# Writing out one engine's loop over pairs of groups: TensorE's passes one behind the other

## Chip, core and metric

The kernel runs on one core of a Trainium2 chip. The metric is the device time of the whole program in microseconds (us): median 2250.71 us of three runs, 2248.42 to 2252.54.

The engines of a core are TensorE (PE; its weight loads are shown apart as PEld), VectorE (DVE), ScalarE (ACT), GpSimd (POOL) and SyncE (SP, which here only issues transfers). Each has an instruction stream of its own; they meet in semaphores.

## What is computed

Four graph layers on 128 boards of 64 tokens with 256 features, everything in float32. Before each layer: layer norm, then ReLU; after each: a residual.

```
h = relu(layernorm(x));  x = x + attention8(h, adj)     # 8 heads, six with static masks, two with adj|eye
h = relu(layernorm(x));  x = x + attention4(h, adj)     # 4 heads, all masked by adj
h = relu(layernorm(x));  x = x + gated(h, adj)          # 4 heads: tanh(where(adj, e @ Wh.T, 0)) @ Wh, relu, gate
h = relu(layernorm(x));  x = x + attention4(h, adj)

attention(h):  softmax(where(mask, q @ k.T * scale, -big)) @ v @ Wo + bo
gated(h):      ha = relu(A @ Wh) @ A_w.T;  hf = h @ fc_w.T
               c = sigmoid(hf @ g1_w.T + ha @ g2_w.T + gbias);  hf * c + ha * (1 - c)
```

## The kernel before

Four boards (256 tokens) are a group, so there are 32 groups. Two groups are in work at once, in two slots: slot 0 takes the even groups, slot 1 the odd ones. A pair of groups is one turn, and there are ITERS = 16 turns. The big matrix products are made of three products of rounded halves (w_hi, w_lo and the same split of the activations), which is why TensorE has so many matmuls; all of them come from one helper line, 437, the transposes from 505, 581 and 714.

What one group goes through is a list of 109 steps (STEPS): for each of the four layers bn, stats, norm, turn (transposes), q, k, v, scores, softmax, and so on; the gated layer (number L2) has r, e, h, s2, a, ah, hp, ha, hf, hat, g, sum. Every engine walks through this list in a function of its own, `step(slot, what, counts)`, and does its share of the step. The two slots are out of phase: slot 1 lags by some 50 steps. How many steps of slot 1 follow each step of slot 0 on an engine is a table written by hand (ORDER).

`passes` runs this on an engine. Its inner `turn` does one pass over the 109 steps of slot 0 and, mixed in, the last `lag` steps of slot 1's group before and the first ones of its group now. The first turn is written out. The other 15 are a hardware loop, `eng.Fori`, in which the semaphore values to wait for depend on the turn and sit in registers (`Counts` with `eng.snap`; register arithmetic, recorded under many lines, works them out). After the loop the rest of slot 1's last group is written out. The five engines each have such a loop, and the code of a turn on TensorE is by far the longest.

The place at which a turn of TensorE ends and the next one begins matters here: the last thing in a turn is step r of the gated layer in slot 1 (six matmuls ps<-hT,u_vec), the first in the next are steps e (matmuls ps<-hT,w_hi and ps<-hT,w_lo), of slot 1 too. At that time slot 0 ends its group: VectorE writes the finished rows (line 1028, into xn), SyncE then issues the transfer of x for the slot's next group (line 350) and the store of the finished one (line 380), and VectorE's bn (line 931) reads the new x. From bn the chain goes over stats (lines 938, 941), the power on GpSimd (line 410) and norm (line 949) to TensorE's transposes (line 505).

The names: hT is the activation after norm and ReLU, transposed; wide holds e; rs and row_terms are small terms of the gated layer; probs the attention's probabilities; xn the normed rows or, at the end of a group, the result; ps is PSUM.

Of the kernel before, what the change touches and what calls it, by code (L numbers as in the profile page):

```python
# [62 lines left out]
def constants():  # L63
# [22 lines left out]
    for part in (0, LO):  # L86
# [13 lines left out]
ORDER = {  # L100
# [5 lines left out]
    "act": (57, (  # L106
# [33 lines left out]
def build(nc, x_in, adjq_in, adjt_in, mats_in, cols_in, rows_in, cst_in, out):  # L140
    GROUPS = x_in.shape[0] // TOK
    ITERS = GROUPS // SLOTS
# [6 lines left out]
    with ctx:  # L149
# [153 lines left out]
                       ("g", L2, 0), ("g", L2, 1), ("sum", L2, 0)])  # L303
        STEPS = att_steps(0) + att_steps(1) + L2_STEPS + att_steps(2)

        def passes(eng, step, order):

            n = len(STEPS)  # L310
            lag, merge = order
            assert len(merge) == n and sum(merge) == n

            def turn(first, now, before):
                done = 0
                for k in range(n):
                    step(0, STEPS[k], now)
                    for done in range(done + 1, done + merge[k] + 1):
                        if done > lag:
                            step(1, STEPS[done - lag - 1], now)  # L320
                        elif not first:
                            step(1, STEPS[n - lag + done - 1], before)

            turn(True, Counts(0), None)
            if ITERS > 1:
                with eng.Fori(0, ITERS - 1) as i:
                    turn(False, Counts(i + 1, eng.snap), Counts(i, eng.snap))
            last = Counts(ITERS - 1)
            for k in range(n - lag, n):
                step(1, STEPS[k], last)  # L330
# [63 lines left out]
        def _(pool):  # L394
# [33 lines left out]
            for s in range(SLOTS):  # L428
                last = nc.gpsimd.memset(RS[s][:, 0:TOK].bitcast(F32), 0.0)
            last.then_inc(setup["terms_zero"], 1)  # L430
            passes(pool, step, ORDER["pool"])


        @block.tensor
        def _(pe):
# [285 lines left out]
            def step(s, what, v):  # L721
# [3 lines left out]
                else:  # L725
                    att(s, k, a, i, v)

            passes(pe, step, ORDER["pe"])


        @block.scalar
        def _(act):
# [32 lines left out]
            def att(s, k, a, i, v):  # L765
# [12 lines left out]
                elif k == "v":  # L778
                    act.wait_ge(sm["v_ps"], n)
                    fn(V[s][:, :, :], bank(s, 3), ACT.Copy).then_inc(sm["v_sb"], 1)  # L780
                elif k == "max":

                    u, m, j, cj = i
                    act.wait_ge(sm["rowmax"], v.eight[u])
                    for b in range(NB):
                        at, row = (cj * NB + b) * SQ, m * NB + b
                        p = PR[s][:, j, at:at + SQ]
                        last = fn(p, p, ACT.Exp, bias=ROWMAX[s][:, row:row + 1], accum_out=ROWSUM[s][:, row:row + 1])  # L788
                    last.then_inc(sm["exp"], 1)
                elif k == "pt":  # L790
                    act.wait_ge(sm["pt_ps"], v.six[2 * a + i])
                    us = turned(a)[i]
                    _, _, j, cj = us[0]
                    at = slice(cj * TOK, (cj + len(us)) * TOK)
                    fn(PTS[s][:, j, at], bank(s, 1 - i)[:, at], ACT.Copy).then_inc(sm["pt_sb"], 1)
                elif k == "pv":
                    act.wait_ge(sm["o_ps"], v.six[2 * a + i])
                    fn(OT[s][:, 0, i, :].rearrange("p (t e q) -> p t e q", t=TT, e=2), o_view(s, i), ACT.Copy
                       ).then_inc(sm["oT_hi"], 1)
# [55 lines left out]
            def step(s, what, v):  # L855
# [3 lines left out]
                else:  # L859
                    att(s, k, a, i, v)  # L860

            passes(act, step, ORDER["act"])


# [275 lines left out]
```

## Time and profile before

| | before |
|---|---|
| median of three runs | 2250.71 us (2248.42 to 2252.54) |
| the profiled execution | 2248.06 us, its span 2245.9 us |
| TensorE busy (matmuls) | 2011.9 us, 21228 matmuls |
| VectorE, ScalarE busy | 1445.6 us, 1151.8 us |
| mean granted TensorE clock | 0.967 |
| instruction fetch (queue q8) | 190 packets, 3.11 MB |
| loop turns (15) | 169.3 to 2179.7 us |

A span goes from the first to the last instruction. In lists of groups the words behind the bar are busy time and mean duration, then the idle time before such instructions and what ended it; "issue" is put where the profile sees nothing that was waited for. The granted clock is 1.00 at 2.4 GHz and 0.50 at 1.2 GHz; between these it is the mean of a stretch that has both. A branch at the end of a loop is recorded with its own duration on the sequencer of each engine ("PEldq" is TensorE's).

### The profile page before, as it was taken

To read this page: it belongs to the slowest core of one execution; us is meant where nothing else is said; L and a number is where in the kernel's file an instruction comes from. 1 tells how busy PE (TensorE), PEld (TensorE's weight loads), DVE (VectorE), ACT (ScalarE), POOL (GpSimd) and SP (SyncE) were. 2 spreads that over 40 slices of the span, in tenths; PEclk is the share of its full clock that TensorE was granted. 3 is DMA by queue.
4 is the path that set the end of the run, shared out by engine and by line. 5 is a ranking of instruction groups with operands and counts; after the bars stand their busy time and mean duration, and the time that the engine had idled before them with its cause. 6 is when DMAs were issued, how large, how long until landed. Compare 5 with 4: busy or idle time off the path is not lost.

```text
span 2245.9 us, 53566 instructions
## 1 busy us (share of the span) xinstructions
PE 2011.9 (90%) x21228; PEld 1818.6 (81%) x21228; DVE 1445.6 (64%) x3769; ACT 1151.8 (51%) x3862; POOL 192.2 (9%) x203
## 2 busy tenths in 40 slices
PE   6699989899898989989899998989989899998997
PEld 5588878788887888878788887888888788887885
DVE  4466667667666667667666666666757666666663
ACT  3355555455455555555455454545455455455552
POOL 0000101100001100100110000100101100000100
PEclk8799999999999999999999999999999999999998
DMA  5000000000000000000000000000000000000000
GB/s 174 1 3 12 12 12 12 11 5 9 12 12 12 11 11 2 11 12 11 12 11 2 12 11 12 11 11 2 11 12 11 11 12 2 12 11 12 11 6 5
DMA packets 40630, 30.66 MB, mean 14 GB/s; under 512 B 15664, under 2 KB 40240, under 8 KB 40432
## 3 DMA queue, kind: packets, MB, share of 16 engines
q1 hardware_dynamic: 40432, 27.48, 4.1%
q8 instruction: 190, 3.11, 0.6%
q14 instruction: 8, 0.07, 0.0%
HBM read 19.08 MB, written 8.39 MB: 12 GB/s over the span
## 4 chain that ended last, share of the span: by engine, by line
PE 62%; issue 18%; DVE 12%; ACT 4%; POOL 4%; DMA 1%; DVEq 0%; SPq 0%; POOLq 0%; ACTq 0%
PE ps L437 57%; PE ps L505 4%; POOL small L410 3%; DVE small L931 2%; DVE xn L949 2%; PE ps L581 2%; ACT probs L788 1%; DVE x L1028 1%; DVE wide L1053 1%; DVE f L1062 1%; POOL x L423 1%; DVE aT L870 1%; ACT f L824 1%; ACT wide L816 1%; DVE small L938 1%
## 5 line engine op out<-in xcount | busy, mean ns | idle before, releaser
L437 PE MATMUL ps<-hT,w_hi 128*128 128x256 f32 x2560 | 511.2, 291 | 55.8 <-issue 47.7
L437 PEld LDWEIGHTS ps<-hT,w_hi 128*128 128x128 f32 x2560 | 420.5, 194 | 73.1 <-issue 50.8
L788 ACT ACTIVATE probs<-probs,small 128x64 f32<-128x64 f32 x1024 | 342.1, 339 | 33.2 <-DVE small L1009 31.4
L437 PE MATMUL ps<-hT,w_lo 128*128 128x256 f32 x1280 | 343.1, 288 | 0.0
L437 PEld LDWEIGHTS ps<-hT,w_lo 128*128 128x128 f32 x1280 | 249.2, 195 | 2.7
L437 PE MATMUL ps<-w_hi,hT 128*128 128x256 f32 (+1 forms) x1024 | 249.1, 312 | 0.0
L410 POOL TENSOR_TENSOR small<-small,consts 128x2 f32<-128x2 f32 x128 | 88.8, 694 | 1776.2 <-DVE small L941 1776.2
L437 PE MATMUL ps<-w_hi,oT 128*128 128x256 f32 x768 | 189.2, 311 | 27.4 <-DVE oT L870 27.4
L437 PE MATMUL ps<-wide,w_hi 128*128 128x256 f32 x1024 | 213.1, 285 | 0.2
L788 ACT ACTIVATION_READ_ACCUMULATOR probs<-probs,small 128x1 f32 x1024 | 196.2, 192 | 0.0
L816 ACT ACTIVATE wide<-ps,c_vec 128x256 fp32r<-128x256 f32 x256 | 107.6, 472 | 148.3 <-PE ps L437 148.3
L437 PEld LDWEIGHTS ps<-w_hi,hT 128*128 128x128 f32 x1024 | 175.4, 188 | 8.4
L1053 DVE SCALAR_TENSOR_TENSOR wide<-ps,c_vec,wide 128x256 fp32r<-128x256 f32 x256 | 109.5, 479 | 103.6 <-ACT wide L816 103.5
L437 PEld LDWEIGHTS ps<-w_hi,oT 128*128 128x128 f32 x768 | 147.5, 211 | 32.5 <-DVE oT L870 32.3
L437 PEld LDWEIGHTS ps<-wide,w_hi 128*128 128x128 f32 x1024 | 163.4, 188 | 3.1 <-DVE wide L870 0.7
L949 DVE TENSOR_SCALAR xn<-x,small 128x256 f32<-128x256 f32 x256 | 123.3, 523 | 62.0 <-POOL small L410 59.7
L437 PE MATMUL ps<-w_hi,cT 128*128 128x256 f32 x768 | 159.3, 290 | 0.3 <-ACT cT L848 0.3
L505 PE MATMUL ps<-consts,xn 128*128 128x128 f32 x512 | 116.3, 324 | 46.1 <-DVE xn L949 42.9
L437 PE MATMUL ps<-w_lo,hT 128*128 128x256 f32 (+1 forms) x512 | 149.9, 310 | 0.0
L763 ACT ACTIVATE hT<-ps 128x256 fp32r<-128x256 f32 x256 | 88.4, 383 | 98.5 <-PE ps L505 97.6
L505 PEld LDWEIGHTS ps<-consts,xn 128*128 128x128 f32 x512 | 62.5, 151 | 86.9 <-DVE xn L949 74.2
L437 PE MATMUL ps<-wide,w_lo 128*128 128x256 f32 x512 | 131.8, 280 | 0.0
(123 smaller groups left out, 4342.5 us busy)
## 6 DMA issues: line engine op xcount, KB each, us to landing
raw_mats<-mats SPq DMA_DIRECT2D x8, 1024.0 KB, 11.9
x<-x SPq DMA_DIRECT2D x32, 256.0 KB, 3.0
out<-xn SPq DMA_DIRECT2D x32, 256.0 KB, 3.0
adj<-adjq SPq DMA_DIRECT2D x64, 16.0 KB, 2.0
adjT<-adjt SPq DMA_DIRECT2D x64, 8.0 KB, 2.1
raw_consts<-board_consts SPq DMA_DIRECT2D x1, 451.5 KB, 3.1
raw_rows<-rows SPq DMA_DIRECT2D x1, 256.0 KB, 4.5
bias_cols<-cols SPq DMA_DIRECT2D x1, 6.0 KB, 3.6
```

The lines of the kernel that those rows point to most:

```text
L410: nc.gpsimd.tensor_tensor(RSTD[s], VE[s], HALF.broadcast_to([P, TT]), ALU.pow).then_inc(sm["rstd"], 1)
L423: nc.gpsimd.tensor_tensor(X[s][:, :], X[s][:, :], F[s][:, 0:512], ALU.add).then_inc(sm["x_ha"], 1)
L437: return nc.tensor.matmul(o, lhsT, rhs, start=start, stop=stop, skip_group_check=True)
L505: last = nc.tensor.transpose(bank(s, H_BANKS[c])[:, t * P:t * P + P], XN[s][:, t * D + c * P:t * D + c * P + P], IDENT)
L581: last = nc.tensor.transpose(bank(s, 1 - i)[:, at:at + P], PR[s][:, j, at:at + P], IDENT)
L763: fn(HT[s][:, 0, c, :], bank(s, H_BANKS[c])[:, 0:TOK], ACT.Relu).then_inc(S[s]["hT_hi"], 1)
L788: last = fn(p, p, ACT.Exp, bias=ROWMAX[s][:, row:row + 1], accum_out=ROWSUM[s][:, row:row + 1])
L816: last = fn(e_view(s, 0, oc, i), e_bank(s, E_BANKS[i], oc), ACT.Identity, bias=CVEC[:, oc, i:i + 1])
L824: fn(tanh_buf(s, i), bank(s, 2 + i), ACT.Tanh).then_inc(sm["tanh"], 1)
L931: nc.vector.bn_stats(STATS[s][:, t, :], X[s][:, t * D:t * D + D]).then_inc(S[s]["bn"], 1)
L949: ts(XN[s][:, t * D:t * D + D], X[s][:, t * D:t * D + D], MV[s][:, t, 0:1], RSTD[s][:, t:t + 1], ALU.subtract, ALU.mult).then_inc(S[s]["xn ...
L1053: stt(e_view(s, 1, oc, i), e_bank(s, E_BANKS[i], oc), CVEC[:, oc, i:i + 1], e_view(s, 0, oc, i).bitcast(F32), ALU.add, ALU.subtract).then_ ...
```

## The change

`passes` gets an argument. For TensorE the 15 turns behind the first are written out one behind the other by a loop in Python; the semaphore values of each turn are then constants. The other four engines keep their hardware loops.

```diff
-        def passes(eng, step, order):
+        def passes(eng, step, order, unrolled=False):
...
             turn(True, Counts(0), None)
-            if ITERS > 1:
+            if unrolled:
+                for i in range(1, ITERS):
+                    turn(False, Counts(i), Counts(i - 1))
+            elif ITERS > 1:
                 with eng.Fori(0, ITERS - 1) as i:
                     turn(False, Counts(i + 1, eng.snap), Counts(i, eng.snap))
             last = Counts(ITERS - 1)
...
-            passes(pe, step, ORDER["pe"])
+            passes(pe, step, ORDER["pe"], unrolled=True)
```

TensorE's program goes from 1367 rows of the listing to 10256, and its lines move by 3 (437 is 440 now). On the other four engines no row differs but for the line numbers.

TensorE at the end of a turn of the loop, before; what stands behind the branch is the code after the loop, and the branch goes back to the same steps of the next turn:

```order
L437 MATMUL ps<-bias_rows,sel_rows 128x256
L437 MATMUL ps<-hT,u_vec 36x256 [waits hT_hi_1]
L437 MATMUL ps<-hT,u_vec 36x256
L437 MATMUL ps<-hT,u_vec 36x256 [waits hT_hi_1]
L437 MATMUL ps<-hT,u_vec 36x256
L437 MATMUL ps<-hT,u_vec 36x256 [waits hT_lo_1] x2
L326 REGISTER_ALU
L326 COMPARE_AND_BRANCH
L437 MATMUL ps<-hT,w_hi 128x256
L437 MATMUL ps<-hT,w_lo 128x256
```

The same place now, where the second turn ends and the third begins:

```order
L440 MATMUL ps<-bias_rows,sel_rows 128x256
L440 MATMUL ps<-hT,u_vec 36x256 [waits hT_hi_1]
L440 MATMUL ps<-hT,u_vec 36x256
L440 MATMUL ps<-hT,u_vec 36x256 [waits hT_hi_1]
L440 MATMUL ps<-hT,u_vec 36x256
L440 MATMUL ps<-hT,u_vec 36x256 [waits hT_lo_1] x2
L440 MATMUL ps<-hT,w_hi 128x256
L440 MATMUL ps<-hT,w_lo 128x256
L440 MATMUL ps<-hT,w_hi 128x256
```

The register addition and the branch between the turns are no longer there; the matmuls and their waits stand as they did.

Inside a turn, on TensorE before step scores (q times k) of slot 0, before the change:

```order
L437 MATMUL ps<-w_lo,hT 128x256
L437 MATMUL ps<-w_hi,hT 128x256 x2
L560 REGISTER_ALU
L437 MATMUL ps<-kT,qT 64x64 [waits q_sb_0,k_sb_0]
L437 MATMUL ps<-kT,qT 64x64 x15
```

Such register rows, which work out the value of a wait, are gone in the same way at all places of the turn.

## Rows read from the trace of the kernel before

**Rows 1.** The page, busy time and share of the span by engine.

```profile
PE 2011.9 (90%) x21228; PEld 1818.6 (81%) x21228; DVE 1445.6 (64%) x3769; ACT 1151.8 (51%) x3862; POOL 192.2 (9%) x203
```

**Rows 2.** What TensorE waited for: total us, times, longest; then the group.

```profile
PE ps L437 <- issue: 50.0, 18, 3.8
...
L437 PE MATMUL ps<-hT,w_hi 128*128 128x256 f32 x2560 | 511.2, 291 | 55.8 <-issue 47.7
```

**Rows 3.** Line 326 (the loop): count, ns min/median/max, first and last start.

```profile
L326 PEldq COMPARE_BRANCH  x15: 83/3434/3934, 299.0 to 2179.7; - x15
...
L326 ACTq COMPARE_BRANCH  x15: 40/45/45, 295.2 to 2176.0; - x15
...
L326 DVEq COMPARE_BRANCH  x15: 50/56/67, 305.3 to 2182.5; - x15
```

**Rows 4.** DMA queues, 573 to 701.6 us: packets, MB, share of 16 engines.

```profile
q8 instruction: 10, 0.16, 0.5%
```

**Rows 5.** Five turns of the loop: stretch, length, busy by engine (instructions), clock, DMA.

```profile
169.30:299.00 129.70, 121.67 (x1319) 110.22 (x1317) 89.06 (x235) 70.68 (x240) 11.86 (x12) 0.99 0.03 10
299.00:435.20 136.20, 124.07 (x1317) 112.83 (x1316) 88.97 (x235) 70.79 (x240) 11.85 (x12) 0.96 0.03 10
435.20:568.50 133.30, 121.74 (x1319) 110.08 (x1317) 88.97 (x235) 70.67 (x240) 11.85 (x12) 0.99 0.04 10
...
967.90:1100.40 132.50, 120.52 (x1319) 108.81 (x1317) 88.96 (x235) 70.50 (x240) 11.86 (x12) 1.00 0.04 10
1100.40:1237.50 137.10, 125.17 (x1319) 113.89 (x1317) 89.13 (x235) 70.81 (x240) 11.85 (x12) 0.95 0.03 10
```

**Rows 6.** Timeline around the end of turn 3: start, us, engine, line, idle before.

```profile
567.90 0.87 PE L437 MATMUL ps<-hT,u_vec 128*36 128x256 f32 x6
...
568.81 0.47 ACT L811 ACTIVATE rs<-ps,s 36x256 fp32r<-36x256 f32 x1 [2.60 <-PE ps L437]
568.94 0.38 SPq L350 DMA_DIRECT2D x<-x  x1
...
572.08 0.36 PE L437 MATMUL ps<-hT,w_hi 128*128 128x256 f32 x1 [3.31 <-issue]
...
573.79 0.84 ACT L816 ACTIVATE wide<-ps,c_vec 128x256 fp32r<-128x256 f32 x2 [4.51 <-PE ps L437]
...
574.66 0.88 DVE L1053 SCALAR_TENSOR_TENSOR wide<-ps,c_vec,wide 128x256 fp32r<-128x256 f32 x2 [4.88 <-ACT wide L816]
...
575.45 0.74 DVE L931 BATCH_NORM_STATS2 small<-x 128x6 f32<-128x256 f32 x2
...
578.15 0.87 PE L505 MATMUL ps<-consts,xn 128*128 128x128 f32 x4
```

**Rows 7.** Timeline around the entry of the loop, in the same form.

```profile
168.79 0.86 PE L437 MATMUL ps<-hT,u_vec 128*36 128x256 f32 x6
169.49 0.36 PE L437 MATMUL ps<-hT,w_hi 128*128 128x256 f32 x1
...
169.83 0.40 SPq L350 DMA_DIRECT2D x<-x  x1
...
172.86 0.74 DVE L931 BATCH_NORM_STATS2 small<-x 128x6 f32<-128x256 f32 x2
...
175.56 0.87 PE L505 MATMUL ps<-consts,xn 128*128 128x128 f32 x4
```

**Rows 8.** Tile x on SyncE, 560 to 2200 us: from issue to landing.

```profile
DMA to landing us min/median/max: 2.8/3.0/3.7
```

**Rows 9.** Stretches around the ends of turns 3 and 8, in the form of rows 5.

```profile
563.00:568.50 5.50, 4.92 (x56) 4.57 (x56) 2.89 (x11) 1.80 (x5) 0.69 (x1) 0.69 0.00 0
572.00:578.00 6.00, 5.92 (x48) 5.76 (x48) 3.08 (x10) 2.52 (x6) 0.69 (x1) 1.00 0.05 17
...
1241.30:1247.00 5.70, 5.59 (x34) 5.62 (x35) 2.35 (x8) 1.68 (x4) 0.69 (x1) 0.70 0.01 4
1300.00:1309.00 9.00, 6.87 (x69) 5.99 (x68) 5.73 (x19) 3.29 (x15) 0.69 (x1) 0.81 0.00 0
```

## The prediction, made before the changed kernel ran

> **What bounds the kernel now.** I read the page first. TensorE is busy for 90% of the span, VectorE for 64%, ScalarE for 51%, so the time is TensorE's work plus the moments in which it has none [rows 1]. Then I read what TensorE waited for. The largest item is no other engine: 50.0 us are put down to issue, in 18 waits, and 47.7 us of it stand before one group of matmuls, the hT,w_hi ones [rows 2]. The reader is to see that "issue" here names no semaphore: nothing that the profile follows was late.
>
> The third view says where they sit. The branch that ends a turn of the loop (line 326) is recorded on each engine, 15 times. On ScalarE and VectorE it takes 40 to 67 ns each time. On TensorE it takes 83 ns once, the median is 3434 ns and the longest is 3934 ns [rows 3]. The loop has 15 turns, so 14 branches are taken and the last falls through; the one cheap record is the one not taken. The window of a turn that starts 4.5 us after its branch still has 10 instruction packets (0.16 MB) [rows 4]: some engine streams its code all the time, in a body that it runs again and again. By its length that is TensorE, with 1319 matmuls and 1317 weight loads in a turn beside 240 instructions on ScalarE and 235 on VectorE [rows 5]. So I read the stall as the wait for the block of code to which the branch goes back.
>
> **The change part by part.** Removed: 14 taken branches of TensorE, its register arithmetic, and the counter of its loop. Added: no matmul, no wait; the number of matmuls is the same. The other four engines keep program and order. So I need the price of a boundary with a branch, and of one without.
>
> Both are in the trace. At 567.90 TensorE starts its six u_vec matmuls, the last work of a turn, and the first matmul of the next turn, hT,w_hi, starts at 572.08: 4.18 us [rows 6]. At the entry of the loop the same two groups meet without a taken branch, since the code runs straight into the body: 168.79 and 169.49, 0.70 us [rows 7]. The difference is 3.48 us; times 14 that is **48.7 us**, and it agrees with the 47.7 us of issue and with the branch records.
>
> Is that time on the path? Behind the gap the next turn starts with the e matmuls of slot 1, which wait for nobody in the gap; ScalarE had done its last work (rs, 568.81 + 0.47) and sat idle for 4.51 us until TensorE gave it e, VectorE for 4.88 us [rows 6]. Nobody uses the gap. What is next in line is the transfer of x: issued at 568.94, read by VectorE's bn (L931) at 575.45, 6.51 us later; without the gap that is 3.03 us. Such a transfer lands 2.8 to 3.7 us after its issue, 3.0 in the median [rows 8]. So the cover of x is gone, and it is late by 0 to 0.67 us. At the loop's entry, where this distance is 3.03 us too (169.83 to 172.86), bn ran 3.37 us after hT,w_hi and the transposes (L505) 6.07 us after it, and at 572 also 3.37 and 6.07 [rows 6, 7]: there x was in time. I take 0.1 us on average, near the median, so **-1.5 us** in 14 turns; the ends are 0 and -9.4 us. The store of the finished group, which has to land before norm overwrites XN, moves with it in the same way and cost nothing at the entry, where norm and the transposes weren't late; I put it at 0.
>
> Register arithmetic: whatever it costs TensorE must be in the issue time that isn't before hT,w_hi, 50.0 - 47.7 = 2.3 us [rows 2]. Ends 0 and 2.3 us; I take 0, since these instructions run ahead of a queue of matmuls.
>
> The turns themselves give the other term. Turn 1, which no taken branch opens, takes 129.7 us. Nine turns with a stall take 132.5 to 133.3 us, which is 129.7 + 3.4. Five take 136.2 to 137.1 us, at a granted clock of 0.95 or 0.96 in place of 0.99 [rows 5]. All 14 turns from 299.0 to 2179.7 are 1880.7 us [rows 3]. The extra time of the five is clock. A short turn drops to 1.2 GHz once, in the stretch of single waits before its end (563.0 to 568.5, clock 0.69), and is at 1.00 behind the stall. A long one does the first too, but shows 0.70 right behind the stall (1241.3 to 1247.0) and 0.81 once more in the middle (1300 to 1309) [rows 9]. The lost part is 5.7 x 0.30 = 1.7 us and 9.0 x 0.19 = 1.7 us: 3.4 us per long turn. In front of the first stands the idle of the stall; TensorE busy across the boundary has no reason for it. The second comes in a quiet place of the softmax and appears only in turns that have the first. If all of it goes, 14 turns cost 14 x 129.7 = 1815.8 us, 64.9 us less than now; so the clock's part is 64.9 - 48.7 = **16.2 us** of gain. Its lower end is 0. It can't be excluded that a turn meets two half-speed stretches for other reasons, since the quiet places remain; I keep 3 us of it for two such turns: 13.2 us.
>
> Sum: 48.7 + 13.2 - 1.5 = 60.4 us. The profiled execution took 2248.06 us (span 2245.9 and 2.2 around it), 2.6 below the median of 2250.71. 2248.06 - 60.4 = 2187.7, and on the scale of the median 2190 us.
>
> One rule is against this. The trace has 83 ns for a branch not taken and 3434 ns for the median of TensorE's [rows 3]. The Trainium skill, Advanced Engine Details and Errata, section Control Flow Timing, puts a compare-and-branch at about 108 ns; by that the edit is worth 14 x 0.108 = 1.5 us in place of 48.7. The three other engines agree with the page's order of size; TensorE doesn't.
>
> **The rivals.** *The long turns stay.* The gap goes, but the half-speed stretches arise as often as now, from the quiet places alone: gain 48.7, less 1.5 for x: 2250.7 - 47.2 = 2203.5. For it: the middle stretch isn't at the boundary. Against: turns of both kinds have the same work, and what precedes the extra stretch is the stall. Chance 0.22.
>
> *The other side of the clock, and x.* The new turn of 129.7 us meets a second half-speed stretch each time (14 x 1.7 = 24 us), or x is late by its maximum (9.4): 2250.7 - 64.9 + 23.8 = 2210, with both 2219. Against it: turn 1 has the new form and shows neither. Chance 0.10.
>
> *The stall isn't the branch's.* TensorE would have to wait at this place for its code in any case, and the gap returns as a fetch in straight code: time as before, 2245 to 2251. For it: a price of a tenth of a microsecond for branches elsewhere [rows 3]; the page named above gives that result. Against: the entry at 169.3, where the same body is reached without a branch and without a gap [rows 7]. Chance 0.03.
>
> *Slower.* Straight code is never used twice, so every block of it must come from memory in time: 10 in most of a turn [rows 4], 140 in 14 turns. If each exposed a wait, the gain of 60.4 us is eaten from 60.4 / 140 = 0.43 us per block on; at 1 us per block the kernel takes 2250.7 - 60.4 + 140 = 2330. Against: such blocks are fetched now as well, in the same order, and all that is put down to issue outside the group behind the branch is 2.3 us in the whole span [rows 2]. The Trainium skill, Runtime: NRT & Kernel Launch, section Instruction fetch mechanics, calls the crossing of a block "mostly hidden"; the trace agrees, with those 2.3 us. Chance 0.02.
>
> **How the numbers follow.** My case has 0.60: 2190 us, its own range 2180 to 2199 from the bounds of x (-8), the register work (+2) and the clock (3 back, or a turn with no half-speed stretch, like the one of 132.5 us at clock 1.00, some more). 0.03 are left for below. The range for 8 in 10 takes in the first rival: 2178 to 2208. Something within 0.2% (4.5 us) of 2250.7, about what a measurement of this kernel can tell from no change, has 0.03; slower by more 0.02; faster 0.95.
>
> **What would show it.** In the profile after: no branch records of TensorE; issue before hT,w_hi near 0; the distance from u_vec to hT,w_hi 0.7 us in all turns; turns of 129.7 us; bn 3.4 to 3.9 us after hT,w_hi, the more the later x;  ScalarE and VectorE with the same busy time and less idle. I am wrong if gaps of over 0.4 us before single matmuls turn up along the turn, if the half-speed stretches become more, or if TensorE at the boundary waits for xn.

## The result and the profile after

| | before | changed |
|---|---|---|
| median | 2251.62 us (2248.42 to 2261.88, 4 runs) | 2184.4 us (2181.92 to 2187.6, 4 runs) |
| the profiled execution, its span | 2248.06, 2245.9 us | 2187.6, 2185.4 us |
| mean granted TensorE clock | 0.967 | 0.972 |
| instruction fetch (queue q8) | 190 packets, 3.11 MB | 167 packets, 2.74 MB |

The ratio is 0.9695, with a 95% interval from 0.9659 to 0.973: 67 us less. 2190 us were predicted, in a range from 2178 to 2208. Beside the experiments the kernel before ran again on other chips; one of those runs took 2345.52 us at a clock of 0.822 and is left out of every comparison.

The changed kernel's lines are 3 higher. From its page, the busy time of the engines, the fetch queue and the group that stood behind the branch (busy, mean ns, idle before and what ended it):

```profile
PE 1998.1 (91%) x21228; PEld 1805.9 (83%) x21228; DVE 1444.6 (66%) x3769; ACT 1151.1 (53%) x3862; POOL 192.0 (9%) x203
...
q8 instruction: 167, 2.74, 0.5%
...
L440 PE MATMUL ps<-hT,w_hi 128*128 128x256 f32 x2560 | 499.8, 287 | 8.1 <-ACT hT L766 7.9
```

The idle before this group was 55.8 us with 47.7 of issue [rows 2]; it is 8.1 us, and none of that is issue. The work is the same, VectorE and ScalarE are as busy as before to within about 1 us [rows 1], and 23 packets fewer of code are fetched although the program is longer.

TensorE's waits for the normed rows, before and then in the changed kernel, and its waits put down to issue (total us, times, longest):

```profile
PE ps L505 <- DVE xn L949: 42.9, 59, 4.9
```

```profile
PE ps L508 <- DVE xn L952: 47.6, 72, 4.9
...
PE ps L440 <- issue: 17.9, 34, 0.7
```

The 17.9 us of issue are not a new wait, though the label suggests it: all of them stand before the probsT,v matmuls (step heads), in 34 gaps. In the kernel before, the same matmuls had 2.3 us put down to issue and these 17.0 us to the copy of probsT (the waits of before, in the same form):

```profile
PE ps L437 <- ACT probsT L795: 17.0, 30, 0.6
```

The releaser is inferred, and with the turns written out the inference names it differently; the sum went from 19.3 to 17.9 us.

The place of the old branch, at one of the two replaced boundaries where x came late (timeline: start, us, engine, line, idle before):

```profile
691.82 0.86 PE L440 MATMUL ps<-hT,u_vec 128*36 128x256 f32 x6
692.52 0.28 PE L440 MATMUL ps<-hT,w_hi 128*128 128x256 f32 x1
...
692.86 0.38 SPq L353 DMA_DIRECT2D x<-x  x1
...
696.21 0.75 DVE L934 BATCH_NORM_STATS2 small<-x 128x6 f32<-128x256 f32 x2 [0.33 <-DMA x<-x]
...
698.92 0.77 PE L508 MATMUL ps<-consts,xn 128*128 128x128 f32 x3 [0.54 <-DVE xn L952]
```

From u_vec to hT,w_hi it is 0.70 us, where it was 4.18 [rows 6] and, at the loop's entry, 0.70 [rows 7]. bn follows 3.69 us after hT,w_hi in place of 3.37.

The turns, cut near the boundary in slot 1 (stretch, length, busy by engine with instructions, granted clock, DMA share, GB/s). The cuts are good to some tenths of a microsecond. Taken exactly, from the start of one u_vec group to the next, the 14 turns from 302.74 to 2118.75 us are 129.6 to 129.9 us long, but for one of 129.2 (the third row, the only one at clock 1.00 throughout) and one of 130.2:

```profile
171.30:302.60 131.30, 123.08 (x1317) 111.64 (x1317) 88.40 (x234) 70.80 (x240) 11.84 (x12) 0.97 0.04 10
...
302.70:432.40 129.70, 121.30 (x1318) 109.95 (x1317) 88.97 (x235) 70.63 (x240) 11.84 (x12) 0.99 0.04 10
...
951.50:1081.20 129.70, 120.63 (x1322) 109.16 (x1321) 89.46 (x236) 70.53 (x240) 11.85 (x12) 1.00 0.04 10
```

The mixture of turns of 133 and 136 us [rows 5] is gone. The first turn was 129.6 us before and is 131.3 us here, at a clock of 0.97.

All 14 turns behind the first, cut exactly at the u_vec groups, before and then in the changed kernel:

```profile
298.35:2179.11 1880.76, 1716.54 (x18426) 1555.07 (x18424) 1245.87 (x3277) 990.08 (x3360) 165.99 (x168) 0.98 0.04 10
```

```profile
302.74:2118.75 1816.01, 1698.46 (x18426) 1539.02 (x18424) 1244.69 (x3277) 989.08 (x3360) 165.77 (x168) 0.99 0.04 10
```

They are 64.75 us shorter. 18.1 us of it are time in which TensorE was busy with the same matmuls, the other 46.7 are idle time.

### The profile page after: what moved, and what is told of

It reads as the page before. It is cut to its first block, busy times and chain, and to the rows that moved or that the text cites. A ratio compares the mean times of both kernels' runs of the same rounds, so it can differ in the third digit from the quotient of the medians.

```text
span 2185.4 us, 53025 instructions
## 1 busy us (share of the span) xinstructions
PE 1998.1 (91%) x21228; PEld 1805.9 (83%) x21228; DVE 1444.6 (66%) x3769; ACT 1151.1 (53%) x3862; POOL 192.0 (9%) x203
## 3 DMA queue, kind: packets, MB, share of 16 engines
q8 instruction: 167, 2.74, 0.5%
## 4 chain that ended last, share of the span: by engine, by line
PE 61%; issue 16%; DVE 13%; ACT 4%; POOL 4%; DMA 2%; SPq 0%; DVEq 0%; POOLq 0%; ACTq 0%
PE ps L440 55%; PE ps L508 4%; POOL small L413 3%; DVE small L934 2%; DVE xn L952 2%; PE ps L584 2%; ACT probs L791 1%; DVE x L1031 1%; DMA x<-x 1%; DVE wide L1056 1%; DVE f L1065 1%; DVE small L941 1%; POOL x L426 1%; DVE aT L873 1%; ACT f L827 1%
## 5 line engine op out<-in xcount | busy, mean ns | idle before, releaser
L440 PE MATMUL ps<-hT,w_hi 128*128 128x256 f32 x2560 | 499.8, 287 | 8.1 <-ACT hT L766 7.9
L440 PEld LDWEIGHTS ps<-hT,w_hi 128*128 128x128 f32 x2560 | 412.0, 190 | 22.1 <-ACT hT L766 16.7
L440 PE MATMUL ps<-hT,w_lo 128*128 128x256 f32 x1280 | 336.8, 284 | 0.0
L440 PEld LDWEIGHTS ps<-hT,w_lo 128*128 128x128 f32 x1280 | 243.6, 190 | 2.7
L508 PE MATMUL ps<-consts,xn 128*128 128x128 f32 x512 | 116.3, 322 | 49.9 <-DVE xn L952 47.6
L508 PEld LDWEIGHTS ps<-consts,xn 128*128 128x128 f32 x512 | 61.8, 149 | 92.4 <-DVE xn L952 79.7
```

The costliest lines, as they stand in the source:

```text
L440: return nc.tensor.matmul(o, lhsT, rhs, start=start, stop=stop, skip_group_check=True)
L508: last = nc.tensor.transpose(bank(s, H_BANKS[c])[:, t * P:t * P + P], XN[s][:, t * D + c * P:t * D + c * P + P], IDENT)
```

## Experiments: what does a branch of TensorE cost, and when?

### Four branches in place of 14

```diff
-                for i in range(1, ITERS):
-                    turn(False, Counts(i), Counts(i - 1))
+                with eng.Fori(0, (ITERS - 1) // 3) as j:
+                    for n3 in range(3):
+                        turn(False, Counts(j * 3 + (n3 + 1), eng.snap), Counts(j * 3 + n3, eng.snap))
```

> TensorE keeps a hardware loop, but of 5 turns of the body with three of the kernel's turns in each: 4 taken branches in place of 14, waits against registers as before. My theory (each taken branch waits once for the code it goes back to, 3.48 us, and draws half-speed stretches behind it): 4/14 of the loss remains, 2184.4 + 4/14 x 67 = 2203 us, with 5 branch records of which 4 are over 3 us. Rival (the register arithmetic and the waits against registers cost the time, or the hardware loop as such): as before, 2251 us. Rival (the wait grows with the length of the body, since all of it is fetched anew): three times the wait, 4 x 10 us, 2225 us and more.

Measured: 2208.9 us (2205.53 to 2209.74), ratio to the kernel before 0.9774 (0.9747 to 0.9801); 2203 were expected. The branch records of TensorE (count, ns min/median/max), then a turn without a branch and the next one, which has one at its start:

```profile
L326 PEldq COMPARE_BRANCH  x5: 83/3480/3783, 556.9 to 2137.1; - x5
```

```profile
426.30:556.10 129.80, 121.77 (x1318) 110.20 (x1318) 88.98 (x235) 70.64 (x240) 11.85 (x12) 0.99 0.04 10
556.10:692.50 136.40, 124.31 (x1318) 112.96 (x1317) 89.13 (x235) 70.72 (x240) 11.84 (x12) 0.96 0.04 10
```

The cost goes with the number of branches taken: 4 of the 5 records are dear. A body three times as long has the same stall (3.48 us, where 3.43 stood), so the stall isn't proportional. The registers and the waits against them are all still there, and turns without a branch take 129.8 us with them as they do without: their cost is nil. The rest against the changed kernel, 24.5 us, is 6 us per branch, more than the stall: behind three of the four branches TensorE meets further half-speed stretches. This is in line with the 14 branches. On the chip of this run the kernel before took 2262.13 us and straight code (the run with x in halves, below) 2184.38, which is 5.6 us per branch.

### A branch to code that was just run

```diff
                 for i in range(1, ITERS):
+                    if i > 1:
+                        with eng.Fori(0, 4):
+                            alone(eng)
                     turn(False, Counts(i), Counts(i - 1))
```

`alone` is one semaphore increment without a wait.

> As the changed kernel, but at each of the 14 boundaries stands a hardware loop of 4 turns around one bare semaphore increment: 42 taken branches of TensorE to code that it has just run. My theory (a branch costs when its target is no longer held): a branch record of about 0.1 us, 2184 to 2190 us. Rival (each taken branch of TensorE costs 3.4 us, whatever the distance): 42 x 3.4 us more, 2325 us. Rival (a branch drains TensorE's queue of matmuls): 14 x 0.3 us and more, 2190 us.

Measured: 2229.27 us (2229.03 to 2229.37), ratio 0.9868 (0.9816 to 0.992). From line 328 of this kernel, the new loop:

```profile
L328 PEldq COMPARE_BRANCH  x56: 76/213/360, 297.1 to 2029.7; - x56
```

So a taken branch took 0.21 us here (0.36 at most), and one not taken 0.08. Neither has the price of 3.4 us. The time, though, was 45 us above the changed kernel, and none of my three cases had that. The idle before hT,w_hi is 24.1 us, 1.7 us per boundary for 4 increments and 3 taken branches; the other 21 us go with the clock. These turns take 133.0 to 133.3 us, 129.7 + 1.7 + 1.7: each has two half-speed stretches, where a turn of the changed kernel has one. It seems that an idle of 1.7 us was enough to draw the second, though no run here has this idle without the small branches.

### Shorter bodies of the real turn

In the kernel before, products with low parts are left out in TensorE's helpers (a part of the result's precision goes; the branch record is what is read, and the times, 2225.5 and 2206.46 us of one run each, are not compared). In e_short1, here one of its two helpers:

```diff
-                    mm(o, WHI[:, m, c, oc * P:oc * P + P], HT[s][:, 0, c, :], c == 0, False)
-                    mm(o, WLO[:, m, c, oc * P:oc * P + P], HT[s][:, 0, c, :], False, False)
...
-                    last = mm(o, WHI[:, m, c, oc * P:oc * P + P], HT[s][:, 1, c, :], False, c == DC - 1)
+                    last = mm(o, WHI[:, m, c, oc * P:oc * P + P], HT[s][:, 0, c, :], c == 0, c == DC - 1)
```

> The kernel before (TensorE in a hardware loop) with fewer products: in features_out and tokens_out only the product of the two high parts is made, which leaves out 2 of 3 matmuls there. A turn of TensorE has about 2130 instructions in place of 2700. Only the branch record counts here. My theory without a known size of what is held: between 1350 and 2700 instructions the record falls from 3.4 us to under 0.2 us at once; this one I expect at 3.4 us still. Rival (the wait is proportional to the length of the body): 2.7 us. Rival (the cost is that of going through the loop's registers): 3.4 us for all lengths, in e_short2 too.

> As e_short1, and in steps ha and hp too only the high parts are multiplied: a turn of about 1870 instructions. The Trainium skill, Runtime: NRT & Kernel Launch, section Instruction fetch mechanics, gives TensorE 2048 instructions of its own memory; by it this body would be held and the branch record falls to about 0.1 us, while that of e_short1 stays at 3.4 us. My theory doesn't need that number: if this one is at 3.4 us too, the limit lies lower. Rival (proportional): 2.4 us.

A turn of e_short1 and its branch record, then the same of e_short2:

```profile
293.20:427.00 133.80, 103.57 (x1046) 87.03 (x1044) 89.31 (x235) 70.67 (x241) 11.82 (x12) 0.87 0.04 10
```

```profile
L326 PEldq COMPARE_BRANCH  x15: 83/3420/4755, 293.2 to 2163.9; - x15
```

```profile
293.20:427.00 133.80, 95.09 (x920) 75.49 (x918) 89.69 (x236) 71.11 (x241) 13.14 (x13) 0.84 0.04 11
```

```profile
L326 PEldq COMPARE_BRANCH  x15: 83/3407/3872, 293.2 to 2150.1; - x15
```

Both stay at 3.4 us in the median, with 1046 + 1044 and with 920 + 918 matmuls and weight loads. The stall doesn't grow with the body; and a body under 2048 instructions isn't held: one whole turn of e_short2 (427.9 to 561.6 us) has 1926 rows of TensorE in the trace, its register, semaphore and branch rows included. The second point goes against what was worked out for e_short2 from the Trainium skill's figure.

### Eight lengths in one run

Before the first turn of the changed kernel (its whole time, 4519.65 us in one run, says nothing here):

```diff
+            def filler(n):
+                for _ in range(n):
+                    mm(PS[:, 7, 0:SQ], SELR[:, 0, :], ROWS[:, 0:SQ], True, True)
+
+            with pe.Fori(0, 3):
+                filler(100)
...
+            with pe.Fori(0, 3):
+                filler(850)
```

> As the changed kernel, and before its first turn TensorE goes through eight hardware loops of 3 turns with nothing but small matmuls in them: 100, 200, 300, 400, 500, 600, 700 and 850 matmuls in a body, each with its weight load, so about 200 to 1700 instructions. Only the branch records count. In the run with the tiny loop a taken branch took 0.21 us, with bodies of some 1870 instructions and more it took 3.4 us. My theory (the branch is cheap if the code is still held): 0.2 us up to some length and 3.4 us above it, nothing between. By the Trainium skill, Runtime: NRT & Kernel Launch, section Instruction fetch mechanics, TensorE holds 2048 instructions, and all eight would be cheap; the 3.4 us at 1870 speak against that already. Rival (the stall grows with the length): a rise over the eight. Rival (it comes from the register work or from full queues at the boundary of the real turns): 0.2 us in all eight.

The branches of the first, the third, the last two loops (100, 300, 700 and 850 matmuls):

```profile
L735 PEldq COMPARE_BRANCH  x3: 76/213/237, 66.9 to 109.6; - x3
...
L739 PEldq COMPARE_BRANCH  x3: 76/208/208, 301.5 to 429.5; - x3
...
L747 PEldq COMPARE_BRANCH  x3: 76/208/208, 1538.9 to 1837.5; - x3
...
L749 PEldq COMPARE_BRANCH  x3: 76/3349/3844, 2018.9 to 2381.7; - x3
```

Seven loops have 0.21 us, up to 700 matmuls with their weight loads, some 1400 instructions. The eighth, some 1700, has 3.35 and 3.84 us. Nothing stands in its body but matmuls, no semaphore and no register work but the loop's own counter. It is a step, not a rise. Nor is it a matter of the time between branches: a pass of the 700 matmuls takes 149 us and its branch is cheap, while a turn of e_short2 takes some 132 us and its branch is dear.

The DMA view shows the fetch itself. The last pass of the loop with 700 matmuls (1688.5 to 1837.4 us), then that of the loop with 850 (2204.1 to 2381.6 us):

```profile
DMA packets 0, 0.00 MB, mean 0 GB/s; under 512 B 0, under 2 KB 0, under 8 KB 0
```

```profile
q8 instruction: 8, 0.13, 0.3%
```

The body of 1400 instructions runs a second and a third time without one packet of code; that of 1700 is fetched anew in each pass. This settles the cause: the branch is dear when the code that it goes back to is no longer held, and the limit lies between about 1400 and 1700 instructions.

### Idle alone, without a branch: three lengths

```diff
                 for i in range(1, ITERS):
+                    if i > 1:
+                        for _ in range(62):
+                            alone(eng)
                     turn(False, Counts(i), Counts(i - 1))
```

> As the changed kernel, with straight code throughout, but at each of the 14 boundaries at which the branch stood TensorE first does 62 bare semaphore increments, with no matmul between: an idle of some 3 us that fetches nothing anew and branches nowhere. My theory (the idle itself draws the half-speed stretches): most of what the change gave is gone, 14 x 3.2 us and a clock part on top, 2230 to 2255 us, turns of 133 us and some of 136 us. Rival (the half-speed stretches came from the fetch or the branch): turns of 132.9 us without long ones, 2184.4 + 14 x 3.2 = 2229 us or less, at a mean clock of 0.975. Rival (nobody needs these 3 us of TensorE): 2184 us.

Measured: 2346.1 us (2344.22 to 2349.0), ratio 1.0383 (1.0327 to 1.0438). I had mis-sized the increments; the idle was 9.1 us per boundary:

```profile
L443 PE MATMUL ps<-hT,w_hi 128*128 128x256 f32 x2560 | 529.2, 298 | 135.9 <-issue 127.8 <-ACT hT L769 7.9
```

Against the changed kernel's 2184.4 us, 162 us were lost to 128 us of idle: 34 us of clock (0.945 in the mean of the profiled execution). The direction is that of the theory, the size of the idle isn't that of the stall, so two more runs set it to that size.

> As the changed kernel, with 23 bare semaphore increments of TensorE at each of the 14 boundaries. In the run with 62 of them each stood 0.15 us behind the last and the boundary took 9.3 us, not the 3 us that I had aimed at; 23 make about 3.4 us, the length of the old stall, without a branch and without a fetch out of turn. My theory (the stall costs its own length, and idle of this length draws further half-speed stretches): 2184.4 + 14 x 3.4 = 2232 us and a clock part of 0 to 30 us, so 2235 to 2262 us, with turns of 133.1 and of 136.4 us mixed. Rival (the further half-speed stretches come from the branch): all turns at 133.1 us, 2232 us, mean clock 0.972 or more.

> As the run with 23 increments at each boundary, with 25. With 23 TensorE's idle before hT,w_hi was 44 us in 14 gaps, 3.15 us each, against 3.41 us each in the kernel before, and 12 turns stayed short; with 25 it is 3.45 us, the length of the old stall. If the length of the idle decides over the half-speed stretches behind it: 14 x 0.3 = 4 us more by itself and several long turns of 136.4 us, 2243 to 2262 us, as the kernel before on the same chip. If the branch adds something of its own: 2236.5 + 4 = 2241 us, with two long turns or fewer.

The group behind the boundary, with 23 and with 25 increments:

```profile
L443 PE MATMUL ps<-hT,w_hi 128*128 128x256 f32 x2560 | 506.3, 290 | 52.2 <-issue 44.1 <-ACT hT L769 7.9
```

```profile
L443 PE MATMUL ps<-hT,w_hi 128*128 128x256 f32 x2560 | 519.3, 294 | 56.5 <-issue 48.4 <-ACT hT L769 7.9
```

| kernel | idle there, in 14 gaps | median (lowest to highest) | before on the same chip | ratio (95%) |
|---|---|---|---|---|
| 23 increments | 44.1 us | 2236.54 (2233.84 to 2241.63) | 2257.62 | 0.9922 (0.9894 to 0.995) |
| before | 47.7 us | | 2242.9 to 2269.4 over both chips | |
| 25 increments | 48.4 us | 2256.92 (2252.7 to 2262.16) | 2260.41 | 0.9978 (0.9957 to 0.9998) |

With 25 increments there is no branch of TensorE and no fetch out of turn, and nearly all of the gain is gone, to within 0.2% of the kernel before. And 4.3 us more idle than with 23 cost about 13 to 20 us: the medians are 20.4 us apart, but the two ran on different chips, and measured each against the kernel before on its own chip they are 0.56% apart, 13 us. The rest is in the turns; two of each kernel in a row:

```profile
435.20:568.30 133.10, 121.79 (x1318) 110.16 (x1317) 88.87 (x235) 70.65 (x240) 11.83 (x12) 0.99 0.04 10
568.30:701.40 133.10, 121.78 (x1318) 110.16 (x1318) 88.89 (x235) 70.67 (x240) 11.83 (x12) 0.99 0.04 10
```

```profile
437.90:570.60 132.70, 120.62 (x1318) 108.93 (x1317) 88.92 (x235) 70.51 (x240) 11.86 (x12) 1.00 0.03 10
570.60:707.60 137.00, 124.89 (x1318) 113.70 (x1318) 89.06 (x235) 70.80 (x240) 11.86 (x12) 0.95 0.04 10
```

With 23 increments nearly all turns have one half-speed stretch; one of the 13 turns between two gaps is long, 137.0 us. With 25, at first turns of 132.7 us at clock 1.00 alternate with ones of 137.0 at 0.95, and 8 of the 13 are long (136.1 to 137.2 us) where the kernel before had 5: TensorE is 4 us longer at the same work in the second kind. So idle alone, without a branch, makes such long turns, and their number reacts to tenths of a microsecond of it.

The kernel before shows the same from turn to turn. Its 14 stalls were not equal: the idle before hT,w_hi was 3.23 to 3.81 us. The turns behind the five longest, 3.46 us and more, were long in four cases; behind the nine shorter ones only one was. Two idles that open long turns are these; the one in rows 6, 3.31 us, opens a short one:

```profile
1241.41 0.36 PE L437 MATMUL ps<-hT,w_hi 128*128 128x256 f32 x1 [3.69 <-issue]
...
1378.04 0.36 PE L437 MATMUL ps<-hT,w_hi 128*128 128x256 f32 x1 [3.81 <-issue]
```

More idle doesn't always mean more clock lost, though. Beyond the idle itself, against 2184.4 us, gaps of 1.7 us cost 21 us, gaps of 3.15 us 8, gaps of 3.45 us 24 and gaps of 9.1 us 34. The changed kernel didn't run on the chips of these runs, so a few microseconds of each figure are uncertain; why the second is the smallest stays open.

### The other engines written out too

```diff
-            passes(pool, step, ORDER["pool"])
+            passes(pool, step, ORDER["pool"], unrolled=True)
...
-            passes(act, step, ORDER["act"])
+            passes(act, step, ORDER["act"], unrolled=True)
...
-            passes(dve, step, ORDER["dve"])
+            passes(dve, step, ORDER["dve"], unrolled=True)
```

> As the changed kernel, but ScalarE, VectorE and GpSimd have their turns written out too; only SyncE keeps its loop. My theory: their branches took 40 to 67 ns and none is waited for, so the time is that of the changed kernel within 0.2%, 2180 to 2189 us. Rival (their loops cost time that hides in the chain, as register work before a wait): up to 15 turns x some 0.5 us, 2177 us. Rival (four streams of straight code compete for the fetch and for the transfers): slower, 2190 to 2200 us.

Measured: 2187.53 us (2181.9 to 2191.53), ratio 0.9681 (0.9645 to 0.9717). No gain, as the records of 40 to 67 ns said [rows 3]; a loss can't be told from the spread.

### Is x late?

First the transfer cut short (only 4 of 128 partitions of x are loaded for the later groups, so most rows of the result are wrong), then the load in halves:

```diff
-                    load_x(s, gnext)
+                    sp.dma_start(X[s][0:4, :].rearrange("p (t d) -> p t d", t=TT), x_v[0:4, gnext, :, :]).then_inc(S[s]["x_in"], 16)
```

> As the changed kernel, but of x only the rows of 4 of 128 partitions are loaded for the groups behind the first two, so most of the rows that are computed are old ones; all other work is the same. It takes away the transfer's length, though not its start. My theory: x is late by 0 to 0.7 us at half of the boundaries, so 2180 us, the waits at L508 back to 43 us. Rival (x is in time): 2184 us, the waits at 47 us.

```diff
+                if gnext is not None:
+                    sp.wait_ge(S[s]["res"], now.six[4])
+                    alone(sp)
+                    load_x(s, gnext, 0)
                 sp.wait_ge(S[s]["res"], now.six[5])
                 if gnext is not None:
                     alone(sp)
-                    load_x(s, gnext)
+                    load_x(s, gnext, 1)
...
-                    dve.wait_ge(sm["x_in"], v.dma)
+                    dve.wait_ge(sm[f"x_in{t}"], v.dma)
```

> As the changed kernel, but the load of x goes in two halves with a semaphore each; the first is issued when the first half of the finished group is added up, about 0.8 us earlier than now. My theory (x has lost its cover: TensorE's waits for the normed rows at L508 rose from 42.9 to 47.6 us in total): some 3 to 5 us of it come back, 2180 us. Rival (x is in time, and the 4.7 us are something else): no change, 2184 us.

The waits at L508 with the short transfer; VectorE's own wait for x in the changed kernel, and with the load in halves:

```profile
PE ps L508 <- DVE xn L952: 42.9, 56, 4.9
```

```profile
DVE small L934 <- DMA x<-x: 1.6, 4, 0.5
```

```profile
DVE small L939 <- DMA x<-x: 1.3, 2, 0.8
```

With the short transfer the waits are back at 42.9 us, the figure of before, so the 4.7 us more at L508 do come from x. In time it is 2182.18 us (2180.55 to 2183.83), ratio 0.9653 (0.9625 to 0.9681): at most 2 us under the changed kernel, which the intervals don't separate. The halves gave 2184.38 us (2182.1 to 2186.42), ratio 0.9661 (0.9632 to 0.969), with 46.4 us of waits, where 2180 were expected: a miss. The trace tells more. The first half was issued 1.0 us before the second and landed after 2.0 us in most cases, and at none of the replaced boundaries did VectorE wait for x any more. Its two waits that are left (0.8 and 0.5 us) stand in the middle of a turn, where slot 1 loads its x and the change took nothing away. So at the boundaries x was in time, and no time came back for it. No version here beats the changed kernel by more than its spread.

## Why the prediction was right, point by point

- *The price of the boundary, 48.7 us for 14.* Right: 4.18 us became 0.70 us, as at the loop's entry, and the 47.7 us of issue are 0. That the entry of the loop was a boundary without a branch made the number, and it held to the hundredth at 13 of the 14 boundaries (0.71 at the other). Before, the same distance was 4.09 to 4.67 us, so one boundary stood well for all: the 14 together lost 50.0 us.
- *The cause.* Right in what it says (the wait for code to go back to), and now shown: a branch over some 1400 instructions takes 0.21 us and fetches nothing, over 1700 to three whole turns it takes 3.3 to 3.9 us (4.8 once). The rival "not the branch's" (2245 to 2251 us) is out, and with it for TensorE the 0.108 us of the Trainium skill, Advanced Engine Details and Errata, section Control Flow Timing; that figure has the size of a branch that isn't taken (0.08 us) or goes to held code (0.21 us).
- *The clock, 13.2 of 16.2 us.* Under-sized, by little. The 14 turns went from 1880.8 to 1816.0 us, 64.75 less, where the prediction's upper end was 64.9; with 50.0 us of it for the boundaries, 14.8 are left for the clock (TensorE's busy time fell by 18.1 us, which draws the line between gap and matmul a little differently). The 3 us that I kept back for two turns with a second stretch weren't needed there; in the profiled execution one such stretch falls into the first turn (131.3 in place of 129.6 us), before the replaced boundaries. That the middle stretch "appears only in turns that have the first" held for the kernel before alone. In the changed kernel the one stretch of a turn can stand in either place: the five turns from 1081.2 to 1729.7 us have it in the middle and none before their end, at the same length of turn. A middle and an end of such a turn (clock 0.51 and 1.00):

```profile
1141.50:1145.00 3.50, 3.31 (x43) 2.98 (x39) 1.82 (x5) 1.53 (x4) 0.52 (x1) 0.51 0.02 5
...
1205.00:1210.00 5.00, 3.32 (x51) 2.77 (x52) 3.12 (x13) 1.70 (x5) 0.69 (x1) 1.00 0.01 3
```

- *x, -1.5 us.* Somewhat too large, within its bounds. VectorE waited 1.6 us for x, 4 times, 0.5 at most, but only two of the four (0.33 and 0.50 us) stand at replaced boundaries; the others are slot 1's, in the middle of a turn. With 1816.0 us for 14 turns against the 1815.8 of 14 undisturbed ones, little is left for it. Down the chain TensorE's waits for xn rose by 4.7 us; of that at most 2 us are in the time.
- *Register work, 0.* Right, by the turns of 129.8 us in the run with three turns per body.
- *The sum.* 60.4 us were forecast, from 2248.06 to 2187.7; the profiled execution took 2187.6. To a tenth that is luck: the 14 turns gained 4.3 us more than forecast (64.75 against 60.4), and a slower start of this execution took 4.4 away (the u_vec group of its first replaced boundary starts at 302.74 us, where it was at 298.35). 2.7 us of that lie before the first of these turns. The median is 2184.4, 5.6 below the 2190 on its scale.
- *The rival "the long turns stay"* (2203.5) fell: without the idle there are none, and the runs with 23 and 25 increments show that idle brings them back. *Slower, by late straight code,* fell too: with 34 gaps of issue only before the heads, whose sum didn't grow, no block of code was late in any of the 14 turns, not even with four engines in straight code.
- What I had not priced: the kernel before isn't one number. On the chips of the experiments its runs lay from 2242.9 to 2269.4 us at mean clocks of 0.969 down to 0.957; the changed kernel's, on the chip of the result alone, from 2181.9 to 2187.6. I took the five long turns of one execution as given; others have more.

## What to carry over

A hardware loop cost next to nothing on the engines whose turn is short (40 to 67 ns, and no gain without it), and a stall per turn on the one whose turn is longer than what the engine holds of its code; look at the duration of the branch records per engine, and write out only that engine's turns, or put several turns into one body. If the same boundary is also reached without a branch, at the loop's entry, the trace of before has the price of both. On TensorE count an idle more than once: with each stall of 3.4 us here about 1.1 us more were lost to the clock behind it (14.8 us in 14), and more in other executions.

## What the runs showed of the hardware

- TensorE's taken branch: 0.21 us with up to about 1400 instructions in the body, 3.3 to 3.9 us (4.8 once) with about 1700, 1840, 2090, 2640 and three times that; 0.08 us when not taken. The Trainium skill, Runtime: NRT & Kernel Launch, section Instruction fetch mechanics, gives the size of TensorE's instruction memory as 2048 instructions; the body over which a branch goes back cheaply is shorter here.
- A loop body of about 1400 instructions on TensorE ran again without a single packet of code fetched; one of about 1700 fetched 8 packets (0.13 MB) in a pass.
- One bare semaphore increment behind the other on TensorE: the records start 0.15 us apart, though each is 0.05 us long; two more of them made the gap 0.3 us longer.
- 0.3 us more of idle in a gap of 3.15 us cost 0.9 to 1.5 us per turn, by the comparison on each chip or of the medians; in the profiled executions 8 of 13 turns were then long, where one had been.
- A gap of 1.7 us in each turn cost nearly as much again in clock (the tiny loops: 45 us for 24 us of idle).
